# Weights by matrix, statistics shared with ScalarE, prefixes behind products, and 32 sorted columns in a graph and expert layer

## What is computed

```python
xn = layernorm(x)                                   # 1250 x 512
# graph part: edge weights, softmax by source node
e = exp(edge_weight - max(0, max(edge_weight)))
att = e / (segment_sum(e, src) + 1e-6)[src]
M = xn @ Wm + bm                                    # 512 -> 256
h = concat([segment_sum(att * M[dst], src), segment_sum(att * M[src], dst)]) @ W1 + b1
g = where(row_sum > 0, relu(relu(layernorm(h)) @ W2 + b2), 0)
# mix part, 8 heads of 64
q, k, v = softmax(xn @ Wq.T + bq), softmax(xn @ Wk.T + bk), xn @ Wv.T + bv
mix = (q @ (k.T @ v) / (q * k.sum()).sum() + q) @ Wp.T + bp
x1 = x + g + mix
out = x1 + best_expert(layernorm(x1)) * its probability   # gelu MLP 512 -> 256 -> 512
```

## Time and profile before

| | us |
|---|---|
| median of 3 runs | 648.46 |
| lowest, highest | 648.01, 654.88 |
| the profiled execution | 646.13 |
| its span | 644.3 |

### The profile page before, as it was taken

How to read it: one execution, slowest core, us unless ns; L and a number is a source line. 1 busy time by engine, 2 the same in 40 slices (tenths; PEclk the granted TensorE clock), 3 DMA queues, 4 the chain that set the end, 5 groups by cost and what they waited for, 6 DMA issues and landing times.

```text
span 644.3 us, 9440 instructions
## 1 busy us (share of the span) xinstructions
PE 564.2 (88%) x2650; PEld 403.7 (63%) x2650; DVE 426.0 (66%) x1067; ACT 240.2 (37%) x742; POOL 237.1 (37%) x194
## 2 busy tenths in 40 slices
PE   3809999999998989999999999998998885199992
PEld 0508888888887862455555555556986655178881
DVE  6695767667667769888788788773325455735552
ACT  0504333333551110144444444445323234446550
POOL 0288777877878778100000000000002223435421
PEclk9958999999999999999999999998999865589998
DMA  8910000000000000400000000000000393233310
GB/s 203 374 35 2 3 2 2 4 2 1 3 2 3 1 2 1 145 2 2 1 1 2 2 2 1 2 2 0 1 1 1 144 401 137 51 103 111 114 53 13
DMA packets 15606, 31.11 MB, mean 48 GB/s; under 512 B 8534, under 2 KB 9165, under 8 KB 14533
## 3 DMA queue, kind: packets, MB, share of 16 engines
q1 hardware_dynamic: 8229, 23.13, 10.3%
q0 software_dynamic: 7328, 7.37, 6.4%
HBM read 24.82 MB, written 7.40 MB: 50 GB/s over the span
## 4 chain that ended last, share of the span: by engine, by line
PE 80%; DVE 14%; issue 2%; DMA 1%; ACT 1%; POOL 0%; SPq 0%; DVEq 0%; POOLq 0%; ACTq 0%
PE banks L533 24%; PE banks L671 21%; PE banks L803 5%; PE banks L668 5%; PE banks L690 3%; PE banks L488 3%; PE banks L707 3%; DVE chunk_1h L1084 2%; PE banks L748 2%; PE banks L683 2%; DVE hot L866 1%; PE banks L573 1%; PE banks L732 1%; PE banks L604 1%; PE banks L794 1%
## 5 line engine op out<-in xcount | busy, mean ns | idle before, releaser
L422 POOL DMA_INDIRECT slots<-record,row_i x144 | 182.6, 1268 | 77.1 <-issue 77.1
L671 PE MATMUL banks<-d_hot,s_hot 128*125 128x251 f32 x432 | 148.8, 426 | 0.4 <-DVE s_hot L1101 0.4
L1369 ACT ACTIVATE adj<-banks x216 | 79.3, 380 | 125.2 <-PE banks L671 123.8
L429 POOL TENSOR_TENSOR rec<-rec,upd 125x512 f32<-125x512 f32 x10 | 13.1, 1328 | 258.5 <-ACT upd L1415 258.5
L1100 DVE TENSOR_SCALAR d_hot<-cst,ends_f 128x250 f32<-128x250 f32 x216 | 75.5, 350 | 31.7 <-PE banks L671 30.8
L668 PEld LDWEIGHTS banks<-hlf 1*125 1x125 f16 x216 | 27.6, 128 | 74.9 <-issue 74.9
L1101 DVE TENSOR_SCALAR s_hot<-cst,ends_f,table 128x125 f32<-128x125 f32 x216 | 73.6, 341 | 0.0
L671 PEld LDWEIGHTS banks<-d_hot,s_hot 128*125 128x125 f32 x432 | 63.4, 186 | 3.6 <-issue 0.5
L533 PE MATMUL banks<-w_hi,xT_hi 128*125 128x512 f32 (+1 forms) x160 | 60.3, 377 | 0.0
L533 PE MATMUL banks<-w_hi,xT_lo 128*125 128x512 f32 (+1 forms) x160 | 58.6, 366 | 0.0
L533 PE MATMUL banks<-w_lo,xT_hi 128*125 128x512 f32 (+1 forms) x160 | 58.5, 366 | 0.0
(11 more groups left out here) (256 smaller groups left out, 1021.5 us busy)
## 6 DMA issues: line engine op xcount, KB each, us to landing
w_raw<-in_w2f SPq DMA_DIRECT2D x4, 1024.0 KB, 8.5
w_raw<-in_wqkv SPq DMA_DIRECT2D x4, 768.0 KB, 17.4
slots<-record,row_i POOLq DMA_INDIRECT x144, 2.6
rec<-in_x SPq DMA_DIRECT2D x2, 1120.0 KB
x_rows<-rec SPq DMA_DIRECT2D x10, 224.0 KB
w1a<-in_w1f SPq DMA_DIRECT2D x1, 2048.0 KB, 7.8
w1b<-in_w1f SPq DMA_DIRECT2D x1, 2048.0 KB, 15.7
b_sb<-in_b2f SPq DMA_DIRECT2D x1, 2048.0 KB, 21.3
```

The lines of the kernel that those rows point to most:

```text
L422: pool.indirect_dma_start(slots, bass.IndirectOffsetOnAxis(ap=row_i[:, c:c + 1], axis=0), record[:, c, :], None).then_inc(slot_st, 16)
L671: pe.matmul(banks[0:TP, bass.ds(b_in, 1), 0:AW], s_hot[:, c % RB, 0:TP], d_hot[:, c % RB, 0:AW], start=False, stop=True, skip_group_check= ...
L1369: act.activation(adj[:, bass.ds(w, AW)].unsqueeze(1), banks[0:TP, bass.ds(b_out, 1), 0:AW], ACT.Copy).then_inc(win_ok, 1)
```

## The change

- The weights come as three pieces, one for each of q, k and v, each of 4 x 512 columns, `fld` behind the first. ACT and DVE split them by matrix (`high_part(i)`, `low_part(i)`), and only the first pair stands ahead of norm(0); the others stand behind x_copy(0) and xT_split(0). `project(0)` waits for each matrix where it is used.
- DVE takes the statistics of tiles 0 to 5 (DT = 6), four of them between its two first picks. ACT takes those of tiles 6 to 9 at its very start: sum, mean, sum of squares around the mean, variance. A root on a dummy value stands ahead of the real one.
- The chunk tables move into the loop (t = 4), their transpose on PE behind the last context and their copy behind the context copies. The zeroing of `ctxd` moves to t = 1.
- In `project` the first prefix stands behind the q product instead of ahead of it, the second behind v instead of k. On DVE pick(2t+2) stands behind shift q.
- PCOLS is 32: POOL scatters 138 columns, and 32 are sorted.

```diff
-PCOLS = 26
+PCOLS = 32
...
+DT = 6
...
-            sp.dma_start(fld[:, :], fold).then_inc(ld_fold, 16)
-            for k in range(KD):
-                sp.dma_start(w_raw[:, k, :], wqkv[:, k, :]).then_inc(ld_wk[k], 16)
+            for i in range(3):
+                a = i * D
+                sp.dma_start(w_raw[:, :, a:a + D], wqkv[:, :, a:a + D]).then_inc(ld_wm[i], 16)
+                if i == 0:
+                    sp.dma_start(fld[:, :], fold).then_inc(ld_fold, 16)
...
-            pe.wait_ge(own_ok, 1)
-            pe.transpose(bank[3][0:8, 0:TP], of_c[:, 0:4, :].rearrange("p a i -> p (a i)"), ident[0:TP, 0:TP]
-                         ).then_inc(own_ps, 1)
...
-                if t == 0:
-                    pe.wait_ge(w_hi_ok, KD)
-                    pe.wait_ge(w_lo_ok, KD)
-                    pe.wait_ge(at_ok, 1)
-                    pe.wait_ge(foldb_ok, 1)
-                    pe.wait_ge(fold_ok, 2)
-                    pe.wait_ge(pick_ok, 2)
                 g = 2 * t + 2
-                if g < NG:
-                    prefix(g)
                 for b, a, n, free, done in ((3, 0, D, q_got, q_ps), (4, D, D, k_got, k_ps),
                                             (5, 2 * D, D, v_ok, v_ps), (6, 3 * D, MD, m_ok, m_ps)):
                     if t >= 1:
                         pe.wait_ge(free, t)
+                    elif b < 6:
+                        pe.wait_ge(w_hi_ok, b - 2)
+                        pe.wait_ge(w_lo_ok, b - 2)
+                    if t == 0 and b == 4:
+                        pe.wait_ge(foldb_ok, 1)
+                    if t == 0 and b == 5:
+                        pe.wait_ge(fold_ok, 2)
+                    if t == 0 and b == 6:
+                        pe.wait_ge(pick_ok, 2)
                     split_product(bank[b][0:TP, 0:n],
                                   [((xT_hi[:, t % 2, k, :], xT_lo[:, t % 2, k, :]),
                                     (w_hi[:, k, a:a + n], w_lo[:, k, a:a + n])) for k in range(KD)]).then_inc(done, 1)
-                    if b == 4 and g + 1 < NG:
+                    if b == 3 and g < NG:
+                        prefix(g)
+                    if b == 5 and g + 1 < NG:
                         prefix(g + 1)
...
+            pe.wait_ge(own_ok, 1)
+            pe.transpose(bank[5][0:8, 0:TP], of_c[:, 0:4, :].rearrange("p a i -> p (a i)"), ident[0:TP, 0:TP]
+                         ).then_inc(own_ps, 1)
...
+            norm_stats(0)
+            norm_stats(1)
+            pick(0)
+            norm_stats(2)
+            norm_stats(3)
+            pick(1)
+            finish_lot(0)
+
+
+            def chunk_tables():
...
+            norm_stats(4)
+            norm_stats(5)
+            dve.wait_ge(stat_ok, DT)
+            for t in range(DT):
                 dve.bn_aggr(mv[:, t, :], stat[:, t, :]).then_inc(var_ok, 1)
 
-            for t in range(NT + 1):
-                if t < NT:
-                    norm_stats(t)
-                if t >= 1:
-                    norm_var(t - 1)
-            dve.wait_ge(fold_ps, 2)
-            dve.tensor_copy(bias("m"), bank[4][0:TP, 0:MD]).then_inc(foldb_ok, 1)
-            dve.wait_ge(own_ps, 1)
-            dve.tensor_copy(at_i[:, 0:TP], bank[3][0:8, 0:TP]).then_inc(at_ok, 1)
-            for k in range(KD):
-                dve.wait_ge(w_hi_ok, k + 1)
-                dve.tensor_tensor(w_lo[:, k, 0:WN], w_raw[:, k, :], w_hi[:, k, 0:WN], ALU.subtract).then_inc(w_lo_ok, 1)
-            for i in range(2):
-                dve.wait_ge(fold_hi, i + 1)
-                dve.tensor_tensor(w_lo[:, 2 * i:2 * i + 2, WN:WP], bank[(5, 7)[i]][:, :].rearrange("p (k n) -> p k n", k=2),
-                                  w_hi[:, 2 * i:2 * i + 2, WN:WP], ALU.subtract).then_inc(fold_ok, 1)
-
-
+            def low_part(i):
+                dve.wait_ge(w_hi_ok, i + 1)
+                a = i * D
+                dve.tensor_tensor(w_lo[:, :, a:a + D], w_raw[:, :, a:a + D], w_hi[:, :, a:a + D],
+                                  ALU.subtract).then_inc(w_lo_ok, 1)
+
+            low_part(0)
             dve.wait_ge(std_ok, 1)
...
-            dve.memset(v_sb[:, :, :, 128:129], 1.0)
-            own_step(dve.memset(ctxd[:, :, :], 0.0))
-            dve.engine_nop().then_inc(ctxd_zero, 1)
+            low_part(1)
+            dve.wait_ge(fold_ps, 2)
+            dve.tensor_copy(bias("m"), bank[4][0:TP, 0:MD]).then_inc(foldb_ok, 1)
+            low_part(2)
+            for i in range(2):
+                dve.wait_ge(fold_hi, i + 1)
+                dve.tensor_tensor(w_lo[:, 2 * i:2 * i + 2, WN:WP], bank[(5, 7)[i]][:, :].rearrange("p (k n) -> p k n", k=2),
+                                  w_hi[:, 2 * i:2 * i + 2, WN:WP], ALU.subtract).then_inc(fold_ok, 1)
+            own_step(dve.memset(v_sb[:, :, :, 128:129], 1.0))
...
+                shift(0, "q", q_sb[:, t, :], q_ps, q_got)
                 if g < NG:
                     pick(g)
-                shift(0, "q", q_sb[:, t, :], q_ps, q_got)
                 shift(1, "k", k_sb[:, r, :], k_ps, k_got)
+                if t == 1:
+                    own_step(dve.memset(ctxd[:, :, :], 0.0))
+                    dve.engine_nop().then_inc(ctxd_zero, 1)
+                if t == 4:
+                    chunk_tables()
                 if g + 1 < NG:
                     pick(g + 1)
...
+            dve.wait_ge(own_ps, 1)
+            dve.tensor_copy(at_i[:, 0:TP], bank[5][0:8, 0:TP]).then_inc(at_ok, 1)
...
+            act.wait_ge(ld_x[1], 32)
+            for t in range(DT, NT):
+                last = act.activation(q_sb[:, t, :], rec[:, t, 0:D], ACT.Copy, accum_out=x_sum[:, 0, t - DT:t - DT + 1])
+            last.then_inc(sum_ok, 1)
+            act.wait_ge(sum_ok, 1)
+            act.activation(mv[:, DT:NT, 0], x_sum[:, 0, :], ACT.Copy, scale=1.0 / D)
+            act.activation(x_sum[:, 1, :], x_sum[:, 0, :], ACT.Copy, scale=-1.0 / D).then_inc(sum_ok, 1)
+            act.wait_ge(sum_ok, 2)
+            for t in range(DT, NT):
+                last = act.activation(q_sb[:, t - DT, :], rec[:, t, 0:D], ACT.Square, bias=x_sum[:, 1, t - DT:t - DT + 1],
+                                      accum_out=x_sum[:, 2, t - DT:t - DT + 1])
+            last.then_inc(sum_ok, 1)
+            act.wait_ge(sum_ok, 3)
+            act.activation(mv[:, DT:NT, 1], x_sum[:, 2, :], ACT.Copy, scale=1.0 / D).then_inc(var_ok, 1)
+
...
+            def high_part(i):
+                act.wait_ge(ld_wm[i], 16)
+                a = i * D
+                act.activation(w_hi[:, :, a:a + D], w_raw[:, :, a:a + D], ACT.Copy).then_inc(w_hi_ok, 1)
+
+            high_part(0)
+            act.activation(std[:, 0:1], const("eps")[0:TP, :], ACT.Sqrt).then_inc(sum_ok, 1)
+            act.wait_ge(sum_ok, 4)
+            act.wait_ge(var_ok, DT + 1)
             act.activation(std[:, :], mv[:, :, 1], ACT.Sqrt, bias=const("eps")[0:TP, :]).then_inc(std_ok, 1)
+            high_part(1)
...
+            high_part(2)
+            act.wait_ge(fold_ps, 1)
+            for i in range(2):
+                act.activation(w_hi[:, 2 * i:2 * i + 2, WN:WP], bank[(5, 7)[i]][:, :].rearrange("p (k n) -> p k n", k=2),
+                               ACT.Copy).then_inc(fold_hi, 1)
```

More of the change, by code:

```diff
@@ L215, in build @@
         rstd = sb("rstd", [TP, NT])
+        x_sum = sb("x_sum", [TP, 3, NT - DT])
         factors = sb("factors", [TP, NT, 4])
@@ L295, in build @@
         ld_wp, ld_w1, ld_b2, ld_bias2 = sem("ld_wp"), sem("ld_w1"), sem("ld_b2"), sem("ld_bias2")
-        ld_wk = [sem(f"ld_wk{k}") for k in range(KD)]
+        ld_wm = [sem(f"ld_wm{i}") for i in range(3)]
         ld_w2k = [sem(f"ld_w2k{i}") for i in range(4)]
@@ L609, in ao_turn @@
                 pe.wait_ge(ao_ok, t + 1)
+                if t == 0:
+                    pe.wait_ge(at_ok, 1)
                 if t == 1:
@@ L912, in finish_lot @@
                                          ALU.add).then_inc(lot_ok, 1)
[L914 to L939, removed]
             def norm_stats(t):
@@ L957, in _ @@
[L957 to L965 removed]
+            dve.wait_ge(slot_zero, 16)
@@ new lines, in _ @@
+            norm_stats(0)
[6 more added lines that the diff above has]
+            def chunk_tables():
+                ends = prs[:, 1:2, :].to_broadcast([TP, 2, NB])
+                chunks = const("chunks")[0:TP, :].unsqueeze(2).to_broadcast([TP, 2, NB])
+                dve.tensor_tensor(of_b[:, 1, :, :], ends, chunks, ALU.is_le)
+                dve.tensor_tensor(of_b[:, 2, :, :], ends, chunks, ALU.is_equal)
+                own_step(dve.scalar_tensor_tensor(of_b[:, 3, :, :], ends, -1.0, chunks, ALU.add, ALU.is_equal))
+                own_step(dve.tensor_reduce(of_c[:, 1:4, :], of_b[:, 1:4, :, :], X, ALU.add))
+                dve.tensor_copy(bank_i[:, 0, :], of_c[:, 1, :])
+                dve.tensor_scalar(of_c[:, 4, :], of_c[:, 1, :], float(NB - 1), float(AW), ALU.min, ALU.mult)
+                own_step(dve.tensor_scalar(of_c[:, 2:4, :], of_c[:, 2:4, :], 1.0, None, ALU.min))
```

(24 more changed lines are left out.)

6 lines of the change are left out of this document (2 added, 4 removed).

## The result

| | median us | lowest, highest | runs |
|---|---|---|---|
| before | 648.75 | 642.77, 654.88 | 20 |
| after | 654.15 | 648.86, 658.49 | 20 |

The ratio is 1.0083, 95% interval 1.0055 to 1.0111: some 5.4 us slower, against 1.2 forecast. The profiled execution took 649.8 us with a span of 648.0.

What follows compares the result with a forecast made beforehand. DVE bounds the start, PE the loop and mix, scatter and sort are balanced: -2.45 us at the sort, +3.65 for six columns, +1.2 on the 648.46 median gives 649.7; terms 647 to 652.5, range 645 to 655.

Steps and rivals of the forecast that it cites:

- The start: Up to x_turn(1): DVE and ACT work before it shrinks, so it starts at 35.1 instead of 48.47, 13.4 us earlier.
- a table load 1.28: First step of ACT's chain, counted from x's arrival at 19.6; with the sums and squares, high_part(0) ends at 29.4.
- Tile 0: x_turn(1) to x_turn(2): 15.15 us plus 1.75 for half clock, against 15.28 before; x_turn(2) at 52.0, 11.75 earlier.
- The sum: Whole kernel: -13.4 start, +1.6 tile 0, +8.7 waits, +0.6 tables, +3.65 for six more sorted columns: +1.2 us.
- the step on its wait: Before x_turn(2): PE waits until DVE's split ends, 2.94 us behind the second prefix.
- The loop: Tile loop: PE waits 1.45 us for xT_lo in every iteration, six losing 8.7 in all; chunk tables cost 0.6 more.
- The sort: Sort beside POOL's scatter: starts at 237.3, ends at 265.9 instead of 264.7, 1.2 us later; scatter over near 251.8.
- the condition under which 32 pay: Scatter and sort balance: the six extra sorted columns pay only if the start's gain reaches the sort.
- The reason given for the 2.7: With 26 columns the sort ends near 260.7, the got load lands near 264.6; table 1.5 us earlier, against 1.2 later.
- The wait does not appear: Rival, loop: prefixes are hidden and the start's gain passes on, sort starting at 226.5; 640.9 us, chance 0.08.
- The clock falls in the loop: Rival, loop: PE's clock halves after each of seven waits, 1.75 us each; sort starts at 249.5; 660 us, chance 0.10.
- ACT or the loads are late: Rival, start: slow 2 KB loads, two table loads and slow sums put x_turn(1) at 38 to 39; 652 us, chance 0.12.

Runs made afterwards that it cites:

- The four executions: Profiled executions of the unaltered changed kernel: the first, the repeat and two more; sort table built at 265.49, 268.39, 265.93 and 270.07 us.
- the first execution: First profiled execution of the unaltered changed kernel: 649.8 us, span 648.0, sort table built at 265.49.
- Both ways of taking the wait away: Changed kernel with the second prefix behind k: 642.65 us; changed kernel with xT_split and norm ahead of the second pick on DVE: 641.86 us.
- the run with 26: Changed kernel with 26 sorted columns instead of 32, 144 scattered: 649.51 us, ratio 1.0014 to the kernel before.

## Why the prediction was right or wrong

**The start: right in kind, 0.3 to 1.9 us too careful.** The four executions have x_turn(1) at 33.20, 34.01, 33.40 and 34.82 instead of 35.1; ACT's first sum, which waits for x, starts at 19.58, 20.58, 19.96 and 21.38 in the same order (19.6 forecast), so most of their spread is that of the load. From start to start the sums take 0.61 and the squares 0.71 (0.65 each), `low_part(0)` took 2.26 (2.25). What failed was the step "a table load 1.28" on ACT's chain: it ran at 0.74, ahead of the wait for x. So `high_part(0)` ended at 27.8 instead of 29.4. The switch to the root took 1.28 and 0.02, as in the earlier trace rows:

```profile
27.82 1.28 ACT L1331 ACT_TABLE_LOAD   x1
29.12 0.20 ACT L1331 ACTIVATE std<-cst 125x1 f32<-125x1 f32 x1
```

The Trainium skill (ScalarE: Activation LUTs, What ACT_TABLE_LOAD costs) gives some 2.66 us for a switch; by the prediction's own working from it x_turn(1) would have come 2.8 us later than 35.1, at 37.9, later than any of the four. The trace shows no drain behind the load.

**Tile 0: the clock is not one number.** In the first execution PE had full clock between 33 and 51 us, in the others 0.91, 1.00 and 0.81 on average. The sum had 1.75 us for it, with bounds of 0 and 3.4; two executions show no fall at all, the other two have one. x_turn(2) came at 48.97, 50.95, 49.17 and 52.80 (52.0 forecast). There the step on its wait was off: PE waits for norm(2) behind the split, not for the split alone, 1.5 to 2.0 us.

**The loop: right in kind, and it was the term that decided.** Waits of 1.18, 1.62, 1.28, 2.53, 1.56 and 1.63, 9.8 in all; forecast 1.45 each and 0.6 more for the chunk tables, 9.3. The five without the tables average 1.45: 1.56 to 1.63 where L915 takes 0.46 or more, as above, and 1.18 and 1.28 where it takes 0.18. Why L915 differs was not tried. The wait with the tables is 0.5 more than forecast. Iterations took 16.5 to 16.8, and 17.7 with the tables (16.5 and 17.1 forecast): besides the wait each lost some 0.2 us more, for which the sum had nothing. From x_turn(2) to the sort the first execution takes 11.1 us longer than before, and the four between 11.1 and 12.7, against the 9.3 of the sum. Both ways of taking the wait away gave back 8.5 and 9.7 us at the table, near the forecast's own figure for that rival (8.8 below the forecast), and 12.7 and 13.5 in the medians.

**The sort: the number right, partly by errors that cancel.** It started at 236.04 to 241.50 (237.3 forecast), on average 1.2 us earlier than in the two executions of before where 2.45 was forecast; table at 267.5 on average; 266.17 + 1.2 = 267.4 was forecast. The last scatter started at 247.51 to 249.25, where 250.6 was forecast, and the longest scatter under the weight splits took 3.1 us, not the 7.5 of the earlier trace rows that was carried over; at 0.19 us saved per microsecond this is worth less than 1 us. That 26 columns would have done better here was right (2.9 at the table against 2.7), and so was the condition under which 32 pay. The reason given for the 2.7 was not: 26 columns started at 237.3 end, by the prediction's own rates, near 262.7, not 260.7 (23.4 columns until 260.6, the other 2.6 at 0.81), and in the run with 26 the table waited for PE's sort, not for the `got` load. So that the size came out is luck.

**The sum: the mechanism right, the size too small.** The step that failed is the last one, that behind the sort the kernel takes what it took before. At the table the executions seen are on average 1.4 us later (from 0.6 earlier to 4.0 later), near the 1.2 of the sum, though more was gained at the start and more lost in the loop than it has; with such a spread the sign of 1.2 was no safe call. The median is 5.4 later. In the profiles the stretch behind the table is 7.1 us longer on average, at a lower granted clock, which is more than the 4 that the medians leave to it, since both profiles of before are short of its median. Whether the executions behind the medians divide alike stays open, since each kernel was profiled one to four times. The 654.15 lies outside the 647 to 652.5 that the terms gave and inside the 645 to 655, which had room for a clock that falls, but put it into the loop; the 0.83% lie in the "within 1%" that had 0.77.

**Rivals.** "The wait does not appear" did not happen. "The clock falls in the loop": once in two of four executions, not seven times, and only at the wait of 2.5 to 2.7 us that the chunk tables make; by the prediction's last paragraph a loop below full clock was to count against it, and in those two it was below full, at a price of some 1.3 us (a step of 19.06 against 17.88 in the execution with the same wait and full clock, and 0.15 in the next). "ACT or the loads are late": no.

## What to carry to other kernels

When work is moved on the engine that sets the time, follow who waits for what comes behind it on the other engines: a prefix moved one place later was free on PE, and the order on DVE made a wait of it, seven times in each execution. On an engine that serves another, put what is waited for ahead of what nobody waits for; the order of four calls was worth 9.7 us up to the table here and 13 in the medians, and made a version 1.1% faster than the kernel before. Tune a balance of two resources (scatter and sort) after the stage ahead of it has its final time, not together with it.

## What the runs showed of the hardware

**Loads in 2 KB pieces were not slow.** I took 261 GB/s from x, whose pieces are 2 KB. The weights, also in runs of 2 KB after the change, moved faster; the windows after, of which the first two share the time with `fld`, whose runs are 6 KB, and the last is w_k alone or nearly so:

```profile
21.00:23.00 2.00, 2.00 (x7) 1.32 (x7) 1.67 (x3) 1.94 (x7) 0.00 (x0) 0.50 1.03 413
23.00:25.00 2.00, 2.00 (x9) 1.43 (x8) 1.60 (x3) 2.00 (x7) 0.00 (x0) 0.50 1.02 383
24.00:26.60 2.60, 2.60 (x7) 1.89 (x7) 2.09 (x6) 2.57 (x8) 0.00 (x0) 0.50 1.04 385
```

In 6 KB runs they had 424 (22 to 24 us before). So the length of the run alone does not hold x back; x is also loaded in parts of 112 and 13 partitions, and whether that is the reason wasn't tried. The same rows show PE at half clock (0.50) while it is busy throughout (2.00 of 2.00 us).

**The same instructions took 8 us more or less behind the table.** From the table to the last store 370.6 to 378.7 us were seen over fourteen executions of ten kernels whose code is the same there, and 375.5 to 378.7 over four of one kernel; the longer ones had the lower mean granted clock, 0.79 to 0.82 against 0.84 and 0.85 between 430 and 600 us. One profile of a kernel with pauses on PE is no measure of a stage behind them.
